# Linear attention of an early-fusion transformer kernel: from steps of two images to steps of two token tiles

## What is computed

```python
eq, ek = jax.nn.elu(q), jax.nn.elu(k)          # q, k, v = x @ W + b, 16 heads of 16
qn = eq / norm(eq);  kn = ek / norm(ek)        # norm over a head's 16 numbers
kv  = einsum('bhsd,bhse->bhde', kn, v)         # b: image, s: its 69 tokens
ctx = einsum('bhsd,bhde->bhse', qn, kv) / sqrt(16)
```

## Time and profile before

| | us |
|---|---|
| median of 3 runs | 1189.4 (1186.96 to 1189.92) |
| the profiled execution | 1189.71 |
| its span, first to last recorded instruction | 1187.9 |
| `linear_attention` in it, first matmul to last copy | 491.3 to 655.9 |

### The profile page before, as it was taken

How to read it: one execution, slowest core, us unless ns; L and a number is a source line. 1 busy time by engine, 2 the same in 40 slices (tenths; PEclk the granted TensorE clock), 3 DMA queues, 4 the chain that set the end, 5 groups by cost and what they waited for, 6 DMA issues and landing times. The chain is left out here.

```text
span 1187.9 us, 21889 instructions
## 1 busy us (share of the span) xinstructions
PE 979.1 (82%) x6860; PEld 872.0 (73%) x6860; DVE 639.1 (54%) x1431; ACT 575.9 (48%) x1175; POOL 650.1 (55%) x631
## 2 busy tenths in 40 slices
PE   6269699997899999678887799992199999999970
PEld 5258377776688888566665699992199999999970
DVE  1435599993544553299998346543623333333335
ACT  0021377775345554344334455652156666666640
POOL 1115487864345545433343599862157777777750
PEclk9689899996789989878889699995589999999995
DMA  7661344440111111000000700006246666666656
GB/s 256 183 239 49 86 152 158 159 143 36 54 54 55 54 55 54 1 0 0 0 0 1 290 1 15 27 15 239 113 143 209 184 205 190 201 197 200 197 168 229
DMA packets 64749, 136.93 MB, mean 115 GB/s; under 512 B 12361, under 2 KB 26434, under 8 KB 63346
## 3 DMA queue, kind: packets, MB, share of 16 engines
q1 hardware_dynamic: 55698, 113.32, 29.8%
q0 software_dynamic: 4848, 14.72, 3.5%
q10 hardware_dynamic: 4144, 8.16, 1.8%
HBM read 114.01 MB, written 24.39 MB: 117 GB/s over the span
## 5 line engine op out<-in xcount | busy, mean ns | idle before, releaser
L121 DVE CAST place<-place 128x512 fp32r<-128x512 f32 (+3 forms) x188 | 106.3, 604 | 176.6 <-PE moe_down L127 79.6
L2249 POOL TENSOR_TENSOR place<-place,place 128x512 fp32r<-128x512 f32 x84 | 138.0, 1642 | 52.5 <-DVE place L121 46.1
L2275 PE MATMUL moe_up<-place,place 128*128 128x128 f32 x1376 | 163.3, 278 | 0.0
L2275 PEld LDWEIGHTS moe_up<-place,place 128*128 128x128 f32 x1376 | 159.7, 195 | 0.0
L127 PE MATMUL moe_down<-place,place 128*128 128x256 f32 x1008 | 130.9, 286 | 0.0
L127 PEld LDWEIGHTS moe_down<-place,place 128*128 128x128 f32 x1008 | 123.3, 191 | 0.0
L1401 POOL TENSOR_TENSOR place<-place,place 128x384 fp32r<-128x384 f32 x54 | 55.2, 1026 | 96.6 <-ACT place L1315 70.8
L2334 ACT ACTIVATE place<-place 128x2048 f32 x44 | 84.0, 1912 | 44.0 <-PEq L2071 29.9
L2347 ACT ACTIVATE place<-moe_up,place 128x128 f32<-128x128 f32 x344 | 97.2, 365 | 13.3 <-POOL place L2249 12.8
L1504 POOL TENSOR_TENSOR place<-place,place 69x1024 f32<-69x1024 f32 x16 | 30.9, 1928 | 93.1 <-DVE place L167 93.1
L1123 PE MATMUL ff_down<-place,place 128*128 128x256 f32 x486 | 71.7, 294 | 8.4 <-POOL place L1401 5.2
(11 more groups left out here) (269 smaller groups left out, 2140.2 us busy)
## 6 DMA issues: line engine op xcount, KB each, us to landing
place<-w_remainder SPq DMA_DIRECT2D x172, 256.0 KB
place<-in_w_dram SPq DMA_DIRECT2D x4, 4096.0 KB, 12.8
place<-gate_rows SPq DMA_DIRECT2D x24, 384.0 KB, 4.7
place<-in_w_dram SPq DMA_DIRECT2D x16, 512.0 KB, 3.8
w_remainder<-place SPq DMA_DIRECT2D x16, 512.0 KB, 2.9
place<-value_rows SPq DMA_DIRECT2D x64, 64.0 KB, 2.3
place<-choices ACTq DMA_DIRECT2D x5, 768.0 KB, 8.1
place<-in_patches_dram SPq DMA_DIRECT2D x9, 384.0 KB, 3.9
```

The lines of the kernel that those rows point to most:

```text
L121: return eng.tensor_copy(out, x)
L2249: pool.tensor_tensor(lo[f], raw[f], hi[f].bitcast(F32), ALU.subtract).then_inc(h_split, 1)
L2275: last = pe.matmul(p1[u][k // HK][:, (k % HK) * P:(k % HK + 1) * P], ws[u][:, c, k * P:(k + 1) * P], xT[u][:, c, :], start=(c == 0), stop= ...
```

## The change

A step is now a window of two tiles of 128 tokens: w runs over NU = 9 windows (18 tiles, 2304 token places, 2208 of them tokens), written out without hardware loops. The 18 tiles and 32 images share tokens in 49 places (`OWN_SHARES`): most tiles touch three images. Key products are done by such shares: ScalarE copies a tile's values out of PSUM once for each image in it, times a column of zeros and ones (`own_rows`, a new input of 128 x 49 numbers, loaded with the other weights) that keeps only that image's rows; the matmul runs over all 128 rows of keys, and sums of an image that lies in two tiles go on in PSUM. An image pair's mask and context follow once its last tile (`last_tile`) is in.

Work moves too: the leading part of x is cut by ScalarE (`cut_x`) instead of VectorE, and the bias of v is added by TensorE as a matmul of one row of ones with the bias, in plain fp32, instead of by VectorE. Order: on TensorE `project` of both tiles of w, `turn_queries` and `gather_keys` of w-2, `context` of the pairs that end in w-3. On GpSimd the multiply of w, then `stage(w+2)`. On VectorE the mask of the first pair of w-2, `roots(w-1)`, `elu(w)`, other masks, `reduce(w)`, `bias_qk(w+1)`; the 11 operations of `roots` follow each other with nothing between. On ScalarE `exp(w)`, `copy_q(w-2)`, the copies out of w-3, `square(w)`, two `share_values` of w+1, `cut_x(w+2)`.

The diff, cut to its core (waits whose place matters are kept; buffers are now two or three for each tile kind, with `qT` kept for all tokens):

```diff
+OWN_SHARES = [(a, n) for a in range(NT) for n in range(NB) if n * S < (a + 1) * P and (n + 1) * S > a * P]
...
+        self.own_rows = w("own_rows", len(OWN_SHARES))
...
+        U = 2
+        NU = NT // U
+        UW = U * P
...
+        of_tile = [[k for k, (a, n) in enumerate(shares) if a == tile] for tile in range(NT)]
+        last_tile = [max(a for a, n in shares if n // 2 == p) for p in range(NP)]
+        pairs_of = [[p for p in range(NP) if last_tile[p] // U == w] for w in range(NU)]
...
+                for w in range(NU):
+                    pool.wait_ge(rn_done, w + 1)
+                    heads = el[w % 3].rearrange("p t (h w) -> p (t h) w", w=HD)
+                    pool.tensor_tensor(heads, heads, inner(nrm[w % 2].rearrange("p t h -> p (t h)"), HD), ALU.mult).then_inc(n_done, 1)
+                    if w + 2 < NU:
+                        stage(w + 2)
...
+                def project(a):
+                    w, j = divmod(a, U)
+                    if j == 0:
+                        pe.wait_ge(staged, w + 1)
+                    x = [half[w % 2][:, :, j * P:(j + 1) * P] for half in (x_hi, x_lo)]
+                    if a >= 2:
+                        pe.wait_ge(qk_read, a - 1)
+                    for c in range(C):
+                        last = product(pe, pq[a % 2][:, 0:QK], (x[0][:, c, :], x[1][:, c, :]),
+                                       (self.wqk1_hi[:, c, :], self.wqk1_lo[:, c, :]), c == 0, c == C - 1)
+                    last.then_inc(qk_mm, 1)
+                    if a >= 2:
+                        pe.wait_ge(v_read, a - 1)
+                    pe.matmul(pv[a % 2][:, 0:D], ones[0:1, :], self.bv1[0:1, :], start=True, stop=False)
+                    for c in range(C):
+                        last = product(pe, pv[a % 2][:, 0:D], (x[0][:, c, :], x[1][:, c, :]),
+                                       (self.wv1_hi[:, c, :], self.wv1_lo[:, c, :]), False, c == C - 1)
+                    last.then_inc(v_mm, 1)
...
+                def turn_queries(w):
+                    pe.wait_ge(n_done, w + 1)
+                    if w >= 1:
+                        pe.wait_ge(qt_read, w)
+                    for j in range(U):
...
+                            last = pe.transpose(pt[:, c, j * P:(j + 1) * P], el[w % 3][:, j, c * P:(c + 1) * P], self.ident)
+                    last.then_inc(qt_mm, 1)
...
+                def gather_keys(w):
+                    for j in range(U):
+                        a = w * U + j
+                        pe.wait_ge(v_read, a + 1)
+                        for k in of_tile[a]:
+                            n = shares[k][1]
+                            p, b = divmod(n, 2)
+                            first = (a - 1, n) not in shares
+                            if first and b == 0 and p >= 2:
+                                pe.wait_ge(kv_read, p - 1)
+                            for c in range(C):
+                                last = pe.matmul(pkv[p % 2][:, b, c, :], el[w % 3][:, j, D + c * P:D + (c + 1) * P],
+                                                 vm[w % 3][:, j, k - of_tile[a][0], c * P:(c + 1) * P],
+                                                 start=(first and c == 0), stop=((a + 1, n) not in shares and c == C - 1), skip_group_check=True)
+                            if b == 1 and a == last_tile[p]:
+                                last.then_inc(kv_mm, 1)
...
+                def context(p):
+                    pe.wait_ge(kv_read, p + 1)
+                    pe.wait_ge(qt_read, last_tile[p] // U + 1)
+                    if p >= 1:
+                        pe.wait_ge(c_read, p)
...
+                            at = (2 * p + b) * S
+                            last = pe.matmul(pc[:, (c * 2 + b) * S:(c * 2 + b + 1) * S], kvm[p % 3][:, b, c, :], qT[:, c, at:at + S], start=True, stop=True)
...
+                for w in range(NU):
+                    for j in range(U):
+                        project(w * U + j)
+                    if w >= 2:
+                        turn_queries(w - 2)
+                        gather_keys(w - 2)
+                    if w >= 3:
+                        for p in pairs_of[w - 3]:
+                            context(p)
+                for w in (NU - 2, NU - 1):
+                    turn_queries(w)
+                    gather_keys(w)
+                    for p in pairs_of[w - 1]:
+                        context(p)
+                for p in pairs_of[NU - 1]:
+                    context(p)
...
+                        dve.wait_ge(qk_mm, a + 1)
+                        dve.tensor_tensor(qb[:, j, :], pq[a % 2][:, 0:QK], self.bqk1, ALU.add).then_inc(qk_read, 1)
...
+                def roots(w):
+                    dve.wait_ge(reduced, w + 1)
+                    if w >= 2:
+                        dve.wait_ge(n_done, w - 1)
+                    for k in range(RSQRT_PARTS):
+                        ins = rsqrt_part(dve, k, var, nrm[w % 2], tmp)
+                        if k == RSQRT_PARTS - 1:
+                            ins.then_inc(rn_done, 1)
+                        else:
+                            link(ins)
...
+                def mask(p):
+                    dve.wait_ge(kv_mm, p + 1)
+                    if p >= 3:
+                        dve.wait_ge(c_mm, p - 2)
+                    dve.tensor_tensor(kvm[p % 3].rearrange("p b c d -> p (b c) d"), pkv[p % 2][:, :, :, :].rearrange("p b c d -> p (b c) d"),
+                                      spread(self.head_mask, 2 * C), ALU.mult).then_inc(kv_read, 1)
...
+                for w in range(NU):
+                    if w >= 2:
+                        mask(pairs_of[w - 2][0])
+                    if w >= 1:
+                        roots(w - 1)
+                    elu(w)
+                    if w >= 2:
+                        for p in pairs_of[w - 2][1:]:
+                            mask(p)
+                    reduce(w)
+                    if w + 1 < NU:
+                        bias_qk(w + 1)
+                roots(NU - 1)
+                for w in (NU - 2, NU - 1):
+                    for p in pairs_of[w]:
+                        mask(p)
...
+                def cut_x(w):
+                    if w >= 2:
+                        act.wait_ge(v_mm, (w - 1) * U)
+                    act.activation(x_hi[w % 2], self.xT[:, :, w * UW:(w + 1) * UW], ACT.Copy).then_inc(x_cut, 1)
...
+                def share_values(a):
+                    w, j = divmod(a, U)
+                    act.wait_ge(v_mm, a + 1)
+                    if w >= 3 and j == 0:
+                        act.wait_ge(kv_mm, pairs_of[w - 3][-1] + 1)
+                    for k in of_tile[a]:
+                        last = act.activation(vm[w % 3][:, j, k - of_tile[a][0], :], pv[a % 2][:, 0:D], ACT.Copy, scale=self.own_rows[:, k:k + 1])
+                    last.then_inc(v_read, 1)
...
+                def exp(w):
+                    act.wait_ge(qk_read, (w + 1) * U)
+                    if w >= 1:
+                        act.wait_ge(reduced, w)
+                    act.activation(ex, qb, ACT.Relu, scale=-1.0).then_inc(r_done, 1)
+                    act.wait_ge(r_done, w + 1)
+                    act.activation(ex, ex, ACT.Exp, scale=-1.0).then_inc(e_done, 1)
...
+                for w in range(NU):
+                    exp(w)
+                    if w >= 2:
+                        copy_q(w - 2)
+                    if w >= 3:
+                        for p in pairs_of[w - 3]:
+                            copy_out(p)
+                    square(w)
+                    if w + 1 < NU:
+                        share_values(w * U + U)
+                        share_values(w * U + U + 1)
+                    if w + 2 < NU:
+                        cut_x(w + 2)
...
+    a["own_rows"] = np.stack([(t * P + row >= n * S) & (t * P + row < (n + 1) * S) for t, n in OWN_SHARES], 1).astype(np.float32)
```

More of the change, by code:

```diff
@@ L1471, in linear_attention @@
[L1471 to L1477, removed]
@@ L1478, in linear_attention @@
-        per = 2 * RSQRT_PARTS
+        shares = OWN_SHARES
+        of_tile = [[k for k, (a, n) in enumerate(shares) if a == tile] for tile in range(NT)]
+        last_tile = [max(a for a, n in shares if n // 2 == p) for p in range(NP)]
+        pairs_of = [[p for p in range(NP) if last_tile[p] // U == w] for w in range(NU)]
+        most = max(len(of_tile[a]) for a in range(NT))
+        m.at(self.la_at)
+        x_hi, x_lo = ([m.take_rounded(C, UW) for _ in range(2)] for _ in range(2))
+        ex = m.take(U, QK)
@@ new lines, in linear_attention @@
+        el = [m.take(U, QK) for _ in range(3)]
+        vm = [m.take(U, most, D) for _ in range(3)]
+        assert m.pos <= self.early_end
+        m.at(self.work_at)
+        qT = m.take(C, NT * P)
+        kvm = [m.take(2, C, P) for _ in range(3)]
+        qb = m.take(U, QK)
+        nrm = [m.take(U, 2 * HEADS) for _ in range(2)]
+        var, tmp = m.take(U, 2 * HEADS), m.take(U, 2 * HEADS)
+        ones = m.take(P)
```

(30 more changed lines are left out.)

167 lines of the change are left out of this document (45 added, 122 removed).

## The result

The changed kernel takes 1196.88 us, median of 4 runs (1195.76 to 1198.81), the kernel before 1189.24 (1186.96 to 1189.92): ratio 1.0072, 95% interval 1.0055 to 1.0089. It is slower by 7.6 us, or 0.7%, where 1181.5 was forecast with a range up to 1194. The profiled execution took 1195.76, its span 1193.9.

What follows compares the result with a forecast made beforehand. VectorE with GpSimd was taken to bound the linear attention's step, TensorE close behind. After the change, fill, six windows of 15.9 us and end closed the stage at 647.8, not 655.9: 1189.4 - 8.1 = 1181.3, said 1181.5, range 1170 to 1194.

Steps and rivals of the forecast that it cites:

- The ring: Linear attention window: project, turns, first share, mask, roots, multiply, subtract, back to project; 14.6 us, 15.9 with the lower clock.
- Fill and end: Linear attention outside the repeating windows: TensorE starts window 2 at 515.6; after window 8's start at 613.2, stage ends at 647.8.
- The middle: Window 2's start to window 8's: six turns of 15.9 us, 95.4, plus four extra shares, 2.2.
- I let it cost as now, 3 us at the lower level: TensorE's clock after each window's 2.4 us idle: slow for 3 us, adding 1.3 to 1.5 us a window.
- (b): Rival: TensorE at 1.2 GHz for most of `project`; loss up to 14, 1203, middle case 1190 to 1196; chance 0.17.
- point of decision: The slow-clock case decides from 17.3 us a window on: 2.7 us lost in each, 5.4 us at the lower level.
- (a): Rival: clock stays up, windows 3 to 8 keep 2.4 GHz at 14.6 us each; gain 18, 1171.5; chance 0.14.
- (d): Rival: the chain of waits does not bind, work does, 9 x 11 us; gain 20 to 40, 1150 to 1170; chance 0.04.
- (e): Rival: the change does not do what it says, keys waiting on masks in each tile; no size given; chance 0.01.
- (c): Rival: nothing measurable, windows of 16.6 to 17.9 us from dearer multiply, bias matmuls, copies or hand-overs; 1186 to 1193; chance 0.17.
- The two prices with bounds: Forms not in the trace: ScalarE value copy 0.384 to 0.595, taken 0.55; fp32 bias matmul 0.27 to 0.92, taken 0.46.
- The signs named: Right: windows 15 to 17 us apart, idles 2 to 2.5. Wrong: clock below 0.8, multiply over 2.2, windows under 13.

Runs made afterwards that it cites:

- e2: Changed kernel with extra matmuls, results unused, on TensorE ahead of the projections (60 in window 2, 32 in window 3, then 16): 1173.44 us, ratio 0.9890.
- e11: Changed kernel with the bias matmul of v on all 128 rows (weights 1/128) in place of one row: 1173.19 us, ratio 0.9886.
- e4: Changed kernel with 8 in place of 11 chained operations in each root, last refinement left out: 1181.44 us, ratio 0.9953.
- e9: Changed kernel with the one-row bias matmul left out, so v lacks its bias: 1165.87 us, ratio 0.9814.
- e10: Kernel before with one more GpSimd operation, result not used, ahead of each multiply: 1196.88 us, ratio 1.0072.

## Why the prediction was wrong, point by point

**The ring** was right in its members, and in its length at full clock: e2 measured it at 14.6, the number of the sum. The single terms are off by up to 0.3 us and make up for each other: both tiles' projections take 5.84 for 5.6. From the last root's end to TensorE's start there were 4.24 us, 4.39 in the sum, but not in the order of the sum. The elu came first and the multiply behind it (568.37, 568.50; 2.89 for 1.93), then the subtract found the way free. The Trainium skill (SBUF — State Buffer, "two separate sides") says that whichever starts first holds the shared port pair for its whole instruction; the trace agrees: the multiply that started 0.13 us behind the elu took 2.89, and 1.93 where it ran by itself at 650.95. The prediction had put this order at 0.2 us more than the other; the changed kernel's ring never shows the other, so that difference is not measured.

**Fill and end** came out right as sums, in part by luck: window 2 starts at 515.4 (515.6 forecast), but the stage began 1.4 us sooner than forecast and the fill took 25.7 us for 24.5. The end takes 34.3 (34.6), of which the projection of window 8 is 10.7 for 6.9 and all behind it 23.6 for 27.7. The new wait of keys for pair 12's mask behind the last roots is there (the 24 key records of window 7 take 4.20 us).

**The middle** is where it failed: 112.7 us for 97.6. The step was "I let it cost as now, 3 us at the lower level". 1.3 us a window was put in. Over windows 2 to 7 the two tiles' projections take 9.5 us in the mean where they take 5.8 at full clock, so the term was 3.6, up to 4.9. Six times the 2.3 us that were missing is 14 of the 15.1 us that the middle is too long, and the stage is 16.0 us longer than forecast (172.7 for 156.7).

Three things were wrong with the term. First, it was read from one step and the mean of the stage. The kernel before held worse: at 613.78, behind the same idle of 2.32 us, its clock stays low for 7 us.

```profile
613.75:620.75 7.00, 6.96 (x24) 4.85 (x25) 6.65 (x18) 3.74 (x5) 1.52 (x1) 0.51 0.00 0
```

And the idle was not the forecast's 2.4 but 2.7 to 3.4 in windows 5 to 8 and 4.6 to 10.4 in windows 2 to 4. e11, which has those idles and no one-row matmul, still loses 2.3 us a window (7.35 for 5.04), not 1.3. Its ring of 16.3 agrees with the 15.9 + 0.4 of the forecast by luck, as its tiles are cheaper at full clock than the 5.6 taken, and the rest of the ring is 0.4 shorter. Second, the kind of work: behind the idle there now stand two one-row matmuls in each window, a form that no row showed. I bounded its price as work, 0.27 to 0.92, and did not ask what it does to the clock. The 3.6 less the 2.3 of e11, 1.3 us a window, goes with it. Third, e4 shows that the idle and the low clock feed each other: idle brings the lower clock, the clock lengthens the ring.

**The rivals.** (b) was the case, with 0.17 and 1190 to 1203; the range ended at 1194, in the middle of it. Its point of decision held: it sets in at a ring of 17.3, and the ring is 18.8. The Trainium skill (TensorE: Matmul & The Clock Gate, Part 1), by which activity releases the clock, was cited for it: e2 agrees, extra matmuls raised the clock from 0.74 to 0.91. (a) would have been right without the low clock: e2 with its filled windows is at 1173. (d) and (e) have no part in it. Of (c), the multiply on 128 rows takes 1.93 where it runs by itself, as on 69; the bias matmul came near its upper end (next paragraph), but the other matmuls were cheaper than summed, so that it cost the ring 0.2.

**The two prices with bounds.** The copies of values by a column take 0.40 each (three in 1.20), near the low end and not 0.55. The fp32 bias matmul, with the late weight load behind it, costs 0.83 a tile at full clock (2.92 less the 2.09 of e9), nearly twice the 0.46 taken and close to its upper bound of 0.92; with all 128 rows it costs 0.43 (e11).

**The signs named** for a right forecast came in part: GpSimd's multiply waits for the last root, its subtract ends every idle, one idle of 10.4 us stands between windows 1 and 2, and keys wait at the end. The two with numbers did not: only one of six windows starts 15 to 17 us behind the one before, and no idle is between 2 and 2.5 us. Two signs of being wrong came: the clock below 0.8 over the stage, tied to (b), and a multiply over 2.2 us, which here is the shut-out by the elu.

## What to carry to other kernels

Draw the ring through the engines' lists before counting work: the change cut the busiest engine's work in half and still lost, because a subtract stood behind a multiply it did not need. When TensorE's projections move from beside the bounding engine into such a ring, its clock becomes a price, here one paid about twice. Take that price from all low stretches of the trace, not from one. A cheap extra matmul in the gap is worth a try as a test, but the cure is the order.

## What the runs showed that was not expected

A matmul that uses one row of weights costs more than one that uses 128. By itself: a tile takes 2.92 us with it and 2.52 with full rows. In the clock: with the same idles ahead of windows 5 to 8, 2.7 to 3.4 us, the lower level lasts 3.5, 10.25, 13.5 and 14 us with one-row matmuls in the stretch and 3.5, 7, 7 and 7 without (e11). The whole switch, one line and a constant, gave 22 us in the changed kernel. The length of the idle counts too: in the kernel before, idles of 3.9 us (e10) had mostly 7 us at the lower level behind them, where those of 2.3 had mostly 3.5. The mean clock of the stage did not show it, 0.84 and 0.85.
